# A two-layer residual kernel: batch 0 worked by quarters of outputs, its first diagonal on TensorE, batch 1 by pairs of units

## What is computed

```python
# layer 0, per batch b: weight W0 shared, sign mask and coefficient of its own
y = x + x @ W0.T + b0 + coeff[b] * (x @ (2 * mask[b] - 1))
# layer 1: weight W1 shared, low-rank pair of the batch's slot, rank 16
z = y + y @ W1.T + b1 + 2.0 * (y @ A[slot[b]]) @ B[slot[b]]
```

## Time and profile before

| | |
|---|---|
| median of three runs | 378.25 us (375.97 to 378.46) |
| the profiled execution | 376.43 us, its span 374.4 us |
| PE busy | 367.3 us, 98% of the span, 1934 matmuls |
| VectorE busy | 308.8 us, 82% |
| ScalarE busy | 206.4 us, 55% |
| GpSimd busy | 91.2 us, 24% |
| moved by the queues | 94.75 MB, mean 253 GB/s |

### The profile page before, as it was taken

One profiled execution on the slowest core, in us unless ns is written; L12 is line 12 of the kernel. 1 busy time (PEld: TensorE's weight loads), 2 busy tenths in 40 slices (PEclk: granted clock), 3 DMA queues, 4 the chain that ended last, 5 costly groups with the idle time before them and its releaser, 6 DMA issues.

```text
span 374.4 us, 5435 instructions
## 1 busy us (share of the span) xinstructions
PE 367.3 (98%) x1934; PEld 311.9 (83%) x1934; DVE 308.8 (82%) x372; ACT 206.4 (55%) x315; POOL 91.2 (24%) x116
## 2 busy tenths in 40 slices
PE   7999999999999999999999999999999999999996
PEld 7889978887888878888788887888878887888875
DVE  4998899999999899976996779947999668968623
ACT  5483765656664776356651767426672466427520
POOL 1355560544007130035001430023200231001300
PEclk9999999999999999999999999999999999999999
DMA  7999999989449494597917968186953969254003
GB/s 233 393 401 345 393 381 370 338 328 359 175 147 340 159 361 175 166 331 239 406 52 258 337 240 332 49 289 274 348 220 101 348 242 402 88 218 169 0 0 114
DMA packets 32332, 94.75 MB, mean 253 GB/s; under 512 B 3610, under 2 KB 4658, under 8 KB 32306
## 3 DMA queue, kind: packets, MB, share of 16 engines
q1 hardware_dynamic: 29488, 85.73, 63.7%
q10 hardware_dynamic: 2754, 8.66, 5.9%
q0 software_dynamic: 64, 0.01, 0.0%
HBM read 86.00 MB, written 8.39 MB: 252 GB/s over the span
## 4 chain that ended last, share of the span: by engine, by line
PE 94%; DVE 2%; DMA 2%; SPq 1%; issue 1%; ACT 0%; DVEq 0%
PE bank L571 37%; PE bank L512 27%; PE bank L518 14%; PE bank L620 6%; PE bank L582 4%; PE bank L460 2%; PE bank L612 2%; DMA ring_raw<-in_mask 2%; PE bank L467 1%; DVE ring_raw L1027 1%; SPq L299 0%; DVE ring L1037 0%; ACT ring L723 0%; SPq L301 0%; SPq L319 0%
## 5 line engine op out<-in xcount | busy, mean ns | idle before, releaser
L571 PE MATMUL bank<-w_two,y_two 128*128 128x512 f32 x600 | 141.4, 390 | 0.0
L723 ACT ACTIVATE ring<-ring_raw,coeff_neg 128x1024 fp32r<-128x1024 f32 (+1 forms) x68 | 74.9, 1102 | 107.2 <-DVE ring_raw L1027 106.7
L571 PEld LDWEIGHTS bank<-w_two,y_two 128*128 128x128 f32 x600 | 111.7, 188 | 23.5 <-issue 0.2
L512 PE MATMUL bank<-x_two,ring 128*128 128x512 f32 x448 | 112.4, 391 | 0.0
L1027 DVE SCALAR_TENSOR_TENSOR ring_raw<-ring_raw,coeff_two 128x1024 f32<-128x1024 int32 (+1 forms) x68 | 84.9, 1261 | 18.2 <-DMA ring_raw<-in_mask 15.2
L382 POOL TENSOR_TENSOR ring_raw<-ring_raw,ident 128x128 f32<-128x128 f32 x64 | 46.7, 750 | 213.4 <-DMA ring_raw<-in_w 213.3
L512 PEld LDWEIGHTS bank<-x_two,ring 128*128 128x128 f32 x448 | 81.4, 188 | 15.0
L1037 DVE SCALAR_TENSOR_TENSOR ring<-ring_raw,coeff_neg,ring 128x1024 fp32r<-128x1024 f32 (+1 forms) x68 | 83.6, 1236 | 7.4 <-ACT ring L723 6.7
L518 PEld LDWEIGHTS bank<-x_two,ring 128*128 128x128 f32 x448 | 61.2, 190 | 4.0
L518 PE MATMUL bank<-x_two,ring 128*128 128x256 f32 x448 | 63.8, 282 | 0.0
L1144 DVE TENSOR_TENSOR y_two<-y_raw,y_two 128x512 fp32r<-128x512 f32 x42 | 31.3, 767 | 4.9 <-ACT y_two L779 4.7
(11 more groups left out here) (50 smaller groups left out, 239.5 us busy)
## 6 DMA issues: line engine op xcount, KB each, us to landing
ring_raw<-in_w SPq DMA_DIRECT2D x60, 512.0 KB, 7.2
ring_raw<-in_mask SPq DMA_DIRECT2D x60, 512.0 KB, 8.1
x_both<-in_x SPq DMA_DIRECT2D x32, 256.0 KB, 3.9
out<-z_rows ACTq DMA_DIRECT2D x15, 512.0 KB, 7.8
w_raw<-in_w SPq DMA_DIRECT2D x12, 512.0 KB, 12.4
b_raw<-in_lora_b SPq DMA_DIRECT2D x8, 448.0 KB, 3.7
ring_raw<-in_w SPq DMA_DIRECT2D x8, 256.0 KB, 6.7
ring_raw<-in_mask SPq DMA_DIRECT2D x7, 256.0 KB, 6.9
```

Of the source, the lines that this page charges most:

```text
L512: pe.matmul(layer0_bank(b, o)[:, 0:2 * T], w, x_two[:, k // PAIR, :, k % PAIR, :], start=(k == 0), stop=False, skip_group_check=True)
L571: ins = pe.matmul(bank[:], y_two[:, q, k, yp, :], w1_two[wp][:, j, k, :], start=(start and k == 0 and n == 0), stop=False, skip_group_chec ...
L723: act.activation(wc_hi[:, e % RING, lo:hi], sums[:, e % RING, lo:hi], ACT.Identity, bias=coeff_neg[:, b:b + 1]).then_inc(wc_hi_done, 1)
```

## The change

`HALVED` becomes 2. A unit of weights is laid out in memory as (piece n, input tile i, 256 outputs). In batch 0 a unit now holds four input tiles (two pairs, the pieces n) and one quarter of the outputs (256), so a quarter q has two units, 2q and 2q + 1. The PE does, for each quarter, layer 0 of its two output tiles and then layer 1 over these two tiles. In quarter 0 each piece is loaded, split and multiplied by itself, and its diagonal isn't added by GpSimd: four matmuls of the rounded identity (`ident_two`) with the two parts of x put x into the two banks. The units of batches 1 on hold what they held, in the new layout. Layer 0 of batch 1 takes two units at a time, as batches 3 on do. The lists of all engines are reordered. In batch 2 `p_add` moves ahead of an `x_low` and a `weights_sum`.

```diff
-    HALVED = 4
+    HALVED = 2
...
+        def pair(b, u, n=0):
+            if b > 0:
+                return u % HT
+            q = u // PAIR
+            g = q // PAIR if u % PAIR else 1 - q // PAIR
+            return PAIR * g + (1 - n if u == 1 else n)
...
             # block_read
-            if k % HT == HT - 1:
+            if k % HT == HT - 1 or b == 0 and k % PAIR == 1:
                 eng.wait_ge(y_full, y_count(b, k))
+            elif b == 0:
+                eng.wait_ge(block_used, k // PAIR + 1)
             else:
-                eng.wait_ge(block_used, (KT - 2) * b + (k + 1 if k < HT else k))
+                eng.wait_ge(block_used, HT + (KT - 2) * (b - 1) + (k + 1 if k < HT else k))
...
             # SyncE
+            def load_piece(u, n):
+                w0_s = w0_first[u] if n == 0 else w0_in[u]
+                sp.dma_start(slot(w0_at, u)[:, n], w0[pair(0, u, n), 0][:, 0]).then_inc(w0_s, 16)
+                if u > 0 or n > 0:
+                    mask_s = mask_first[u] if n == 0 else ring_in[u]
+                    sp.dma_start(slot(mask_at, u)[:, n], mask[0, pair(0, u, n), 0][:, 0]).then_inc(mask_s, 16)
...
-            for u in range(HT):
-                load_x(0, pair(0, u))
-                load_weights(0, u)
-            for k in range(HT):
-                load_w1(k)
-            for u in range(HT, KT):
-                load_weights(0, u)
-            sp.wait_ge(ids_in, 16)
-            load_lora(0)
-            for k in range(HT, KT):
-                load_w1(k)
+            for g in range(XG):
+                load_x(0, x_pair(0, g))
+                load_piece(g // PAIR, g % PAIR)
+            load_w1(0)
+            load_w1(1)
+            for q in range(1, XG):
+                load_weights(0, PAIR * q)
+                load_weights(0, PAIR * q + 1)
+                if q == XG - 1:
+                    sp.wait_ge(ids_in, 16)
+                    load_lora(0)
+                load_w1(PAIR * q)
+                load_w1(PAIR * q + 1)
             for b in range(1, NB):
-                for u in range(PAIR):
+                early = HT if b == 1 else PAIR
+                for u in range(early):
                     load_weights(b, u)
                 for g in range(XG):
                     load_x(b, g)
-                for u in range(PAIR, RING):
+                for u in range(early, RING):
                     load_weights(b, u)
...
             # GpSimd
-            w0_diagonal(0, PAIR)
-            w0_diagonal(0, PAIR + 1)
-            for k in range(HT):
-                w1_diagonal(k)
+            pool.tensor_copy(ident_two[:], ident[:]).then_inc(ident_two_done, 1)
+            w1_diagonal(0)
+            w1_diagonal(1)
+            w0_diagonal(0, 3)
+            w1_diagonal(2)
+            w1_diagonal(3)
...
-            w0_diagonal(0, KT - 2)
-            w0_diagonal(0, KT - 1)
+            w0_diagonal(0, 5)
+            w1_diagonal(4)
+            w1_diagonal(5)
+            w0_diagonal(0, 7)
+            w1_diagonal(6)
             lora_a_diff(0)
-            for k in range(HT, KT):
-                w1_diagonal(k)
+            w1_diagonal(7)
+            w0_diagonal(1, 0)
             lora_a_low(0)
+            w0_diagonal(1, 1)
             lora_b_low(0, 0)
-            pool.wait_ge(b_lo_done, 1)
-            w0_diagonal(1, 0)
-            w0_diagonal(1, 1)
-            pool.wait_ge(w0_diag, diagonals(1, 1))
             lora_b_low(0, 1)
...
             # TensorE
+            def layer0_first(q):
+                outs = range(PAIR * q, PAIR * (q + 1))
+                if q >= PAIR:
+                    pe.wait_ge(y_lo_done, y_parts(0, PAIR * (q - PAIR) + 1))
+                blocks = [(n, i) for n in range(PAIR) for i in range(PAIR)]
+                if q == 0:
+                    for u in outs:
+                        for n in range(PAIR):
+                            pe.wait_ge(x_lo_done, PAIR * u + n + 1)
+                            if pair(0, u, n) == 0:
+                                pe.wait_ge(ident_two_done, 1)
+                                for o in outs:
+                                    for part in range(2):
+                                        pe.matmul(first_bank(o), ident_two[:], x_two[:, 0, part, o, :], start=False, stop=False,
+                                                  skip_group_check=True)
+                            pe.wait_ge(wc_hi_done, parts(0, u, n))
+                            for part in [[o] for o in outs] if u == 1 and n == 1 else [outs]:
+                                for i in range(PAIR):
+                                    for o in part:
+                                        first_high(u, n, i, o)
+                                pe.wait_ge(wc_lo_done, parts(0, u, n))
+                                for i in range(PAIR):
+                                    for o in part:
+                                        ins = first_low(u, n, i, o)
+                        if u == 0:
+                            ins.then_inc(block_used, 1)
+                    return
+                for u in outs:
+                    pe.wait_ge(wc_hi_done, parts(0, u))
+                    for n, i in blocks:
+                        for o in outs:
+                            first_high(u, n, i, o)
+                pe.wait_ge(wc_lo_done, parts(0, outs[0]))
+                for n, i in blocks:
+                    for o in outs:
+                        ins = first_low(outs[0], n, i, o)
+                ins.then_inc(block_used, 1)
+                pe.wait_ge(wc_lo_done, parts(0, outs[1]))
+                for o in outs:
+                    for n, i in blocks:
+                        first_low(outs[1], n, i, o)
...
             def layer0_half(b, h):
-                if b > FIRST:
+                if b != FIRST:
                     for u in range(HT * h, HT * (h + 1), PAIR):
                         layer0_units(b, (u, u + 1))
                     return
...
-            def layer1_first(h):
-                if h == 1:
-                    low_weights(HT - 1)
-                for k in range(HT * h, HT * (h + 1)):
+            def layer1_first(q):
+                if q > 0:
+                    low_weights(PAIR * q - 1)
+                for k in range(PAIR * q, PAIR * (q + 1)):
                     if k == KT - 1:
+                        low_weights(k - 1)
                         pe.wait_ge(y_lo_done, y_parts(0, k))
                         plain_low_rank(0)
...
-                    if k != HT - 1:
-                        low_weights(k)
+                low_weights(KT - 1 if q == XG - 1 else PAIR * q)
...
             # ScalarE, the new list (the one before is at L824)
             x_high(0, 0)
+            act.wait_ge(coeff_done, 2)
+            x_high(0, 1)
+            weights_high(0, 0, 0)
+            act.dma_start(ids[:], slot_ids).then_inc(ids_in, 16)
+            act.dma_start(b1_raw[:], b1).then_inc(b1_in, 16)
+            weights_high(0, 0, 1)
+            x_high(0, 2)
+            weights_high(0, 1, 0)
+            x_high(0, 3)
             act.wait_ge(fill_done, 2)
             act.activation(h_stack[B_HI:P, :], fill_ones[B_HI:P, :], ACT.Copy).then_inc(stacks_set, 1)
             act.activation(b_stack[B_HI:P, :], fill_zeros[B_HI:P, :], ACT.Copy).then_inc(stacks_set, 1)
+            weights_high(0, 1, 1)
             act.wait_ge(cols_in, 16)
             w1_high(0)
+            y_high_first(0)
+            y_high_first(1)
+            w1_high(1)
             w12_copy(0)
             w12_copy(1)
+            weights_high(0, 2)
+            weights_high(0, 3)
...
+            weights_high(0, 6)
+            weights_high(0, 7)
             lora_a_high(0)
             lora_b_high(0)
+            weights_high(1, 0)
+            w1_high(6)
+            y_high_first(6)
+            y_high_first(7)
+            weights_high(1, 1)
             lora_b_copy(0, 0)
+            w1_high(7)
             lora_b_copy(0, 1)
...
             # VectorE, the new list (the one before is at L1173)
             x_low(0, 0)
             dve.wait_ge(coeff_done, 2)
             weights_sum(0, 0, 0)
+            x_low(0, 1)
             weights_sum(0, 0, 1)
             weights_low(0, 0, 0)
+            weights_low(0, 0, 1)
+            weights_sum(0, 1, 0)
+            x_low(0, 2)
+            weights_low(0, 1, 0)
+            weights_sum(0, 1, 1)
+            x_low(0, 3)
+            weights_low(0, 1, 1)
             dve.wait_ge(cols_in, 16)
             t1_sum(0)
             y_low_first(0)
+            y_low_first(1)
+            weights_sum(0, 2)
             w1_low(0)
             t1_sum(1)
+            weights_sum(0, 3)
+            weights_low(0, 2)
+            weights_low(0, 3)
             w1_low(1)
+            weights_sum(0, 4)
+            t1_sum(2)
             y_low_first(2)
             y_low_first(3)
             w1_low(2)
...
+            weights_sum(0, 7)
+            weights_low(0, 6)
+            weights_low(0, 7)
```

(8 more changed lines are left out.)

189 lines of the change are left out of this document (70 added, 119 removed).

## The result

The changed kernel takes **379.64 us**, the median of seven runs (379.31 to 380.7). The kernel before has 376.87 us over its seven runs of the same comparison (375.97 to 378.46). The ratio is 1.0066, with a 95% interval of 1.0048 to 1.0085: 2.5 us more (1.8 to 3.2). This is slower, by less than 1%. The profiled execution took 379.64 us with a span of 377.5, against 376.43 and 374.4.

What follows compares the result with a forecast made beforehand. The PE, busy 98% of the span, was taken as the bound. Batch 0 +1.8 us and batch 1 -0.2 gave +1.6 on 376.43, 378.0; over half the 1.8 to the median shown made it 379.1, range 375.0 to 382.3.

Steps and rivals of the forecast that it cites:

- Quarter 0: Layer 0 of batch 0's first quarter: VectorE's chain has the last low at 15.9 us; the PE loses 2.5 us.
- The start: First split product, with the second pair's x_high ahead of the first weights_high on ScalarE: +0.2 us, bounds 0 and 0.7.
- the identity: Diagonal by TensorE in quarter 0: four more matmuls of 256 columns, +0.5 us on the PE.
- Quarter 1: PE waits after quarter 0's layer 0: w1_low(0) 0.2 us, unit 3's high 0.3, y_low(2) behind sum(0,4) 0.4.
- Quarter 3: End of batch 0: y_low(6) and w1_low(6) stand behind batch 1's sums on VectorE; the PE waits about 0.6 us.
- Rival B: The lock: four GpSimd adds at 14 to 21 us hold VectorE whole, some 1.2 us more, 380.3 us; chance 0.10.
- Rival C: Batch 1's transfers land late, delaying VectorE from sum(1,1) at batch 0's end: +3.5 us, 382.6 us; chance 0.10.
- Rival A: Quarter 0's VectorE chain runs at its floor, 14.8 us, and later quarters never starve: 376.4 us; chance 0.26.
- Rival D: The order changes nothing, the PE's loss just moves; only +0.5 and -0.2 us: 377.8 us; chance 0.12.
- Batch 1 by pairs: Batch 1's layer 0 by two units at a time: 22.2 us instead of 22.44, -0.2 us.
- Moving p_add: In batch 2, p_add ahead of one x_low and one sum: counted as a move at no cost.
- that cover: Batch 1's x land at 55 to 57 us, wanted from 60; if the cover went, each us is one on the PE.

Runs made afterwards that it cites:

- the trials of the start and of the diagonal: Two edits of the changed kernel: second pair's x_high and x_low behind first weights_high and sums, fills ahead, ratio 1.0046; first diagonal by GpSimd, no identity matmuls, 1.0072.
- the trials: Changed kernel with quarter 3's own work first in VectorE's and ScalarE's lists, ratio 1.0045; without GpSimd's two subtractions for B in batch 0, 1.0023; both, 1.0020.

## Why the prediction was right, and where it was not

**The sign and the mechanism.** The forecast was 379.1 us with a loss that grows by small waits in batch 0, the TensorE otherwise full. Measured are 379.64 and these waits. That the two numbers lie so near is partly luck, and it lies in the level: I added over half of 1.8 us for the median then shown, 378.25, and the median of more runs is 376.87. The effect itself was forecast at +1.6 and is +3.1 in the profiled executions, +2.5 (1.8 to 3.2) in the ratio. On the measured level, 376.87, my effect would have given 378.5.

**Quarter 0: right.** Forecast lost 2.5 us, measured 2.04. The chain through VectorE is what I summed: the last low ended at 15.46 (forecast 15.9), and the fill held the last weights_high back by 0.48 us (forecast 0.5). The start (0.35 against 0.2) and the identity (0.48 against 0.5) are right as marks. My sum lists them as terms of their own, but its 2.5 us are what is left up to a fixed end, so a later start only makes that rest smaller. In the trials of the start and of the diagonal, quarter 0 did not end earlier.

**Quarter 1: right in sum, one term did not come.** With the last matmuls of quarter 0's layer 1, 1.10 us against 0.2 + 0.3 + 0.4 for w1_low(0), unit 3 and y_low(2). The wait for unit 3's high is 0.60 us, since its sum waited for GpSimd's pair of adds. No wait for y_low(2) shows: its sum(0,4) ran at 27.42, about when I had its mask land, and y_low(2) was done at 29.71, wanted at about 29.8 (27.96 and eight matmuls). The adds took 2.21 us beside VectorE, and my sum had no term for them:

```profile
19.18 2.21 POOL L408 TENSOR_TENSOR ring_raw<-ring_raw,ident 128x128 f32<-128x128 f32 x2 [3.40 <-DMA ring_raw<-in_w]
```

VectorE's w1_low(0), which had begun before them and kept its length, and its sum(0,3) behind them:

```profile
18.99 1.22 DVE L1116 TENSOR_TENSOR w_two<-w_raw,w_two 128x1024 fp32r<-128x1024 f32 x1
...
21.50 1.28 DVE L1090 SCALAR_TENSOR_TENSOR ring_raw<-ring_raw,coeff_two 128x1024 f32<-128x1024 int32 x1 [0.42 <-POOL ring_raw L408]
```

**Quarter 3: the mis-sized term.** Forecast 0.6, measured 2.36 us. The order that I wrote down was right, its times were not: sum(1,1) ended at 51.6 (forecast 50.5), w1_low(6) at 54.7 (53.9) and w1_low(7) at 59.2 (56.4). Two things failed. First, what the sums wait for: I said the mask, at 46.6 and 49.3 us, and it was GpSimd, which had eight operations in a row for 7.5 us. My sum has no term for GpSimd there (from 49.3 to 50.5 is the sum of weights alone), where its adds for w1 took 1.45 and 1.55 us against 0.47 alone. Second, I took w1_low(7) and low(1,1) at durations without GpSimd's subtractions. By the trials the order costs 0.8 us, and the subtractions beside VectorE another 1.2 once the order is mended (10.70 - 9.53), 0.9 if it is not (11.50 - 10.61).

**Why the kernel before did not pay for it.** It had the same subtractions, and its sum(1,1) took 2.32 us as well:

```profile
51.83 2.32 DVE L1027 SCALAR_TENSOR_TENSOR ring_raw<-ring_raw,coeff_two 128x1024 f32<-128x1024 int32 x1
```

Yet its TensorE waited for nothing from 30 to 58.7 us. Its layer 0 ended at 44.10, and tile 6 was wanted 28 matmuls of 512 columns later, 6.4 us; y_low(6) and y_low(7) ran at 48.18, and one of the stretched operations more or less did not matter. By quarters, layer 0 of tile 6 ends at 50.51 and the tile is wanted four matmuls later, 0.9 us. The cover that one long layer 1 gave is what the change spends. This is read from the two timelines; no run varied the cover alone.

**Rival B.** The rule of the Trainium skill, "SBUF — State Buffer", section "Who interferes with whom", holds more here than I allowed: that VectorE operations with two inputs in SBUF and GpSimd operations that read SBUF exclude one another. The traces agree. My own row already said so, and I read it wrongly. I compared the stretch of x_low, 0.25 us, with the length of the add, 0.62, when only their overlap counts: the add ran from 14.09 to 14.71 and x_low from 14.31, so 0.25 of 0.40. In quarter 3 low(1,1) began at 54.66 with a subtraction running to 55.89, and lost 1.03 of these 1.23 us; w1_low(7) lost 1.10 of 1.24. But the overlap is VectorE's loss only when GpSimd's operation began first. w1_low(0) in the row above overlapped the adds by 1.02 us and lost nothing: it had begun first, and the first add stretched instead, from 0.47 to 1.34 us. B's price was 1.2 us at 14 to 21 us; what shows there is less, T1's two sums at 0.95 instead of 0.69 us each and the 0.42 us of sum(0,3). That the two subtractions in quarter 3 cost 1.2 us as well is a coincidence.

**Rival C.** Its place was right and its cause wrong: VectorE did stand at sum(1,0) and sum(1,1), for 1.27 and 0.85 us, but for GpSimd. **Rival A** fell because quarter 0's chain had the waits that I counted (the last low at 15.46, not 14.8), and because quarters 1 and 3 starved. **Rival D** is excluded by the interval, whose lower end is +1.8 us.

**Batch 1 by pairs: right.** -0.17 against -0.2 in the kernel after. Moving p_add costs nothing and is needed: without it a wait of 0.31 us appears. The rate of the queues falls to 298 GB/s in batch 1's layer 0 (366 before) with the TensorE full, so that cover held as well.

**Open** is what quarter 0 would take if VectorE had less to do in it, or with the fills alone moved: no run tried it. The spread of the first transfers, up to 0.8 us at the end of quarter 0, is also unexplained.

## What to carry to other kernels

Where the bound engine is full, finer interleaving only helps if the engines behind it have slack inside each small part; a long stretch of the bound engine's work is the cover for their irregular operations, and cutting it into quarters makes each of them count. Cost a small GpSimd operation by what it takes beside a busy VectorE, and count both engines' operations as one list when VectorE's have two inputs in SBUF and GpSimd's read it too. To read a contention from two rows, see first which operation began first; the stretch of the later one is to be compared with the time from its start to the other's end, never with the other's length. And look at the granted clock when a trial comes out worse than its waits.
